# Value products that move 128 columns, and the next unit's pieces at the end of a step

## The reference, cut to what matters

```
L0  graph attention, 2 layers, 8 heads of 32:   out = softmax(leaky(self + neigh) + mask) @ feat
L0  causal attention inside the ffn, 16 heads of 16, and L3 attention, 16 heads of 16:  attn @ v
L1  latent attention, 16 heads, values of 64:   attn @ kv_rope
```

## Time and profile before

| | |
|---|---|
| median of 3 runs | 1486.96 us (1483.61 to 1492.53) |
| the profiled execution | 1486.61 us |
| its span, first to last instruction | 1484.8 us |
| PE busy, PEld busy | 1224.9 us (82%), 1031.5 us (69%) |
| DVE, ACT, POOL busy | 783.6, 595.3, 241.1 us |
| mean granted TensorE clock | 0.836 |
| graph attention's value products, L568 | 512 records, 106.2 us |
| small attention's, L872 | 768 records, 92.6 us |
| latent attention's, L1487 | 512 records, 60.5 us |

### The profile page before, as it was taken

How to read it: one execution, slowest core, us unless ns; L and a number is a source line. 1 busy time by engine, 2 the same in 40 slices (tenths; PEclk the granted TensorE clock), 3 DMA queues, 4 the chain that set the end, 5 groups by cost and what they waited for, 6 DMA issues and landing times. The chain is left out here.

```text
span 1484.8 us, 19438 instructions
## 1 busy us (share of the span) xinstructions
PE 1224.9 (82%) x7064; PEld 1031.5 (69%) x7064; DVE 783.6 (53%) x1966; ACT 595.3 (40%) x1032; POOL 241.1 (16%) x261
## 2 busy tenths in 40 slices
PE   6978888887998979989799799835267897979888
PEld 3546776676785867878589679734257685868777
DVE  2355434444756745544467457464564555744544
ACT  3335333442653733434244244211144553623433
POOL 2100000000404112334200000000023303012332
PEclk9976555656999988989899999966589998978999
DMA  8300000000000012223000000000022000012222
GB/s 331 95 2 2 1 1 1 2 1 0 2 1 1 2 53 76 84 87 100 26 1 1 1 1 2 3 2 4 0 80 63 1 1 0 2 62 75 75 87 79
DMA packets 19406, 52.17 MB, mean 35 GB/s; under 512 B 3504, under 2 KB 5808, under 8 KB 19184
## 3 DMA queue, kind: packets, MB, share of 16 engines
q1 hardware_dynamic: 19312, 50.93, 10.7%
HBM read 49.74 MB, written 1.05 MB: 34 GB/s over the span
## 5 line engine op out<-in xcount | busy, mean ns | idle before, releaser
L1098 POOL TENSOR_TENSOR p_WML<-p_raw,p_WMH 128x768 fp32r<-128x768 f32 (+1 forms) x78 | 135.1, 1735 | 256.9 <-ACT p_WMH L1200 251.3
L190 POOL TENSOR_SCALAR rstds<-mvs 128x4 f32<-128x4 f32 x16 | 3.7, 231 | 733.1 <-DVE mvs L185 484.1
L1258 ACT ACTIVATE p_AHI<-p_A 128x512 fp32r<-128x512 f32 x78 | 49.1, 629 | 177.5 <-DVE p_A L1399 177.4
L568 PEld LDWEIGHTS PS<-p_FT,p_PTS 128*128 128x128 f32 x512 | 105.9, 313 | 19.7 <-DVE p_PTS L748 17.7
L568 PE MATMUL PS<-p_FT,p_PTS 128*128 128x33 f32 x512 | 106.2, 381 | 11.9 <-ACT p_PTS L630 10.3
L79 PE MATMUL PS<-p_WMH,p_AHI 128*128 128x256 f32 x312 | 89.6, 287 | 13.5 <-DVE XS L1369 10.2
L1399 DVE TENSOR_TENSOR p_A<-p_A,PS 128x512 f32<-128x512 f32 x62 | 42.6, 688 | 108.3 <-PE PS L1154 108.0
L1403 DVE TENSOR_TENSOR p_ALO<-p_A,p_AHI 128x512 fp32r<-128x512 f32 x78 | 62.1, 796 | 67.4 <-ACT p_AHI L1258 65.3
L872 PEld LDWEIGHTS PS<-p_V,p_PTS 128*128 128x128 f32 x768 | 93.6, 197 | 0.0
L872 PE MATMUL PS<-p_V,p_PTS 128*128 128x17 f32 x768 | 92.6, 260 | 0.0
L748 DVE COPY p_PTS<-PS 128x512 f32<-128x512 f32 x32 | 22.1, 691 | 131.0 <-PE PS L581 131.0
(11 more groups left out here) (369 smaller groups left out, 3355.6 us busy)
## 6 DMA issues: line engine op xcount, KB each, us to landing
p_raw<-in_moe SPq DMA_DIRECT2D x62, 448.0 KB, 3.2
p_fr<-in_fold SPq DMA_DIRECT2D x16, 512.0 KB, 3.8
p_raw<-in_ffn SPq DMA_DIRECT2D x16, 320.0 KB, 2.9
p_raw<-in_wpack SPq DMA_DIRECT2D x8, 416.0 KB, 7.8
CP<-in_consts SPq DMA_DIRECT2D x1, 1725.0 KB, 12.3
XS<-in_x SPq DMA_DIRECT2D x1, 1024.0 KB, 15.3
out<-XS SPq DMA_DIRECT2D x8, 128.0 KB, 2.6
p_ctr<-in_ctxT SPq DMA_DIRECT2D x1, 512.0 KB, 16.1
```

The lines of the kernel that those rows point to most:

```text
L568: m = pe.matmul(PS[:, 6, hh * 33:hh * 33 + 33], PTS[:, n % 2, hh // 2, (hh % 2) * S + mt * P:(hh % 2) * S + mt * P + P], FT[:, u % 2, 2 * ...
L1098: g.tensor_tensor(WML[:, n % RING, :], raw[:, n % RAW, 0:SEL], WMH[:, n % RING, 0:SEL].bitcast(F32), ALU.subtract).then_inc(s["w_lo"], 1)
```

## The change

Widening: each value product moves 128 columns, with the used 17, 33 or 65 somewhere among them. The moving slice starts at the head's own columns where 128 fit behind them and otherwise ends with them, so the used part lies at the start or at the end of 128 result columns; four products fill one PSUM bank. DVE reads only the used columns. PE's first values wait for both parts of the ones columns, since the slice reaches over other heads.

Pieces: `STEP` is one lower for every piece. PE does `due(n)` at the end of step n instead of its beginning. ACT and DVE do `due(n - 1)` in step n: ACT ahead of `leaky(n + 2)` instead of behind it, DVE right behind `shift(n + 1)`, ahead of the copy of bank 4, instead of behind `elu`.

```diff
-                STEP = {"tr0": 2, "tr1": 3, "t": 4, "s": 5, "f0": 6, "f1": 7}
+                STEP = {"tr0": 1, "tr1": 2, "t": 3, "s": 4, "f0": 5, "f1": 6}
...
                             if n == 0:
-                                pe.wait_ge(s["ones"], 1)
+                                pe.wait_ge(s["ones"], 2)
...
-                                    m = pe.matmul(PS[:, 6, hh * 33:hh * 33 + 33], PTS[:, n % 2, hh // 2, (hh % 2) * S + mt * P:(hh % 2) * S + mt * P + P],
-                                                  FT[:, u % 2, 2 * (t // 2) + mt, 4 * hg + hh, :], start=(mt == 0), stop=(mt == 1))
+                                    lo = 33 * hh if hg == 0 else 33 * (5 + hh) - P
+                                    m = pe.matmul(PS[:, 6, hh * P:hh * P + P], PTS[:, n % 2, hh // 2, (hh % 2) * S + mt * P:(hh % 2) * S + mt * P + P],
+                                                  FT[:, u % 2, 2 * (t // 2) + mt].rearrange("p h o -> p (h o)")[:, lo:lo + P], start=(mt == 0), stop=(mt == 1))
...
                         for n in range(NN):
-                            for u, j in due(n):
-                                job(u, j)
                             if n:
                                 values(n - 1)
                             if n + 2 < NN:
                                 scores(n + 2)
                             weights(n)
+                            for u, j in due(n):
+                                job(u, j)
...
                             exps(n)
+                            if n:
+                                for u, j in due(n - 1):
+                                    if j[0] != "f":
+                                        high(u, j)
                             if n + 2 < NN:
                                 leaky(n + 2)
-                            for u, j in due(n):
-                                if j[0] != "f":
-                                    high(u, j)
...
-                            o = PS[:, 6, 0:132].rearrange("p (h o) -> p h o", h=4)
+                            at = 0 if hg == 0 else P - 33
+                            o = PS[:, 6, :].rearrange("p (h o) -> p h o", h=4)[:, :, at:at + 33]
...
                             if n + 1 < NN:
                                 shift(n + 1)
+                            if n:
+                                for u, j in due(n - 1):
+                                    low(u, j)
                             v.wait_ge(s["pt"], 2 * n + 1)
...
-                            for u, j in due(n):
-                                low(u, j)
...
-                                    at = (2 * qt + hh) * (HD + 1)
+                                    at = (2 * qt + hh) * P
+                                    hd = 2 * hp + hh
+                                    lo = hd * (HD + 1) if hd < 8 else (hd + 1) * (HD + 1) - P
...
-                                        m = pe.matmul(PS[:, 6 + n % 2, at:at + HD + 1], PTS[:, n % 2, hh, c * P:c * P + P],
-                                                      V[:, 2 * j + kt, 2 * hp + hh, :], start=(kt == 0), stop=(kt == qt))
+                                        m = pe.matmul(PS[:, 6 + n % 2, at:at + P], PTS[:, n % 2, hh, c * P:c * P + P],
+                                                      V[:, 2 * j + kt].rearrange("p h d -> p (h d)")[:, lo:lo + P], start=(kt == 0), stop=(kt == qt))
...
-                                        i = pe.matmul(PS[:, 6 + n % 2, at:at + DC + 1], PTS[:, n % 2, c:c + P],
-                                                      KV2[:, 2 * j + kt, DC:2 * DC + 1], start=(kt == 0), stop=(kt == 1))
+                                        i = pe.matmul(PS[:, 6 + n % 2, at:at + P], PTS[:, n % 2, c:c + P],
+                                                      KV2[:, 2 * j + kt, 1:2 * DC + 1], start=(kt == 0), stop=(kt == 1))
```

More of the change, by code:

```diff
@@ L1006, in outputs @@
                             v.wait_ge(s["pv"], n + 1)
-                            o = PS[:, 6 + b, 0:4 * (HD + 1)].rearrange("p (a d) -> p a d", a=4)
+                            at = 0 if hp < NH // 4 else P - HD - 1
+                            o = PS[:, 6 + b, :].rearrange("p (a d) -> p a d", a=4)[:, :, at:at + HD + 1]
                             v.reciprocal(rin[:, b, :], o[:, :, HD]).then_inc(s["rec"], 1)
@@ L1483, in values @@
                                 for hh in range(2):
-                                    at = (2 * qt + hh) * (DC + 1)
+                                    at = (2 * qt + hh) * P
                                     for kt in range(2):
                                         c = qt * 512 + hh * S + kt * P
-                                        i = pe.matmul(PS[:, 6 + n % 2, at:at + DC + 1], PTS[:, n % 2, c:c + P],
-                                                      KV2[:, 2 * j + kt, DC:2 * DC + 1], start=(kt == 0), stop=(kt == 1))
+                                        i = pe.matmul(PS[:, 6 + n % 2, at:at + P], PTS[:, n % 2, c:c + P],
+                                                      KV2[:, 2 * j + kt, 1:2 * DC + 1], start=(kt == 0), stop=(kt == 1))
                             i.then_inc(s["pv"], 1)
@@ L1590, in outputs @@
                             v.wait_ge(s["pv"], n + 1)
-                            o = PS[:, 6 + b, 0:4 * (DC + 1)].rearrange("p (a d) -> p a d", a=4)
+                            o = PS[:, 6 + b, :].rearrange("p (a d) -> p a d", a=4)[:, :, DC - 1:2 * DC]
                             v.reciprocal(rin[:, b, :], o[:, :, DC]).then_inc(s["rec"], 1)
```

## The result

The changed kernel takes 1381.61 us in the median (1380.92 to 1388.97, four runs), against 1489.74 for the kernel before in the same comparison: ratio 0.929, 95% interval 0.9243 to 0.9337. The forecast was 1409, the range 1386 to 1460. The profiled execution of after took 1380.92 us (span 1379.1), 105.7 us less than the profiled one of before.

A forecast was written before the change was run, and what follows sets the result against it. The graph stage was taken as bound by PE at its lower clock, small and latent attention by PE outright. 1486.6 - 96 (graph stage) + 18 (wide records) gave 1409 us, range 1386 to 1460.

The forecast's parts named there:

- The clock: Graph stage: wide value products raise PE's clock to the upper level after about two steps, and it stays.
- Rival 1: Graph stage: clock stays low, only piece waits go (-19 us), bill +18, 1486 us, no change; chance 0.08.
- rival 2: Graph stage: clock flickers, a third to half of 32 steps low, +28 to +46, 1437 to 1455 us; chance 0.15.
- The graph stage: Graph attention: 156 us against 252.4, so -96 us, with plain steps of 4.53 us and two low steps first.
- The move: Graph stage: moving ACT's and DVE's parts of pieces removes PE's waits; the first transposing piece still waits 0.7 us for elu.
- Rival 4: Graph stage: pieces do not gain, waits stay, +17 us, 1426 us; counted within the forecast's chance of 0.65.
- the 1.03 us: Graph step: time PE waits for the copies behind the transposes anyway; a piece costs only what exceeds it.
- both engines were idle where the pieces moved to: Graph stage: ACT and DVE idle there waiting for PE; one PE piece had waited 2.58 us for DVE's L674.
- The bill: Small and latent attention: wide records cost +11.9 and +6.1 us, together +18.0 (2 to 35).
- the stand-in: Wide record's full-clock price, taken from the 256-column fp32r product: 0.120 us, floor 0.107, upper bound 0.133.
- The narrow side: Price of a narrow value record at full clock: 0.1045 us in the small attention, 0.108 in the latent.
- PE has no idle time there: Small and latent attention: both PE-bound, so nothing hides the wide records' +18.0 us.

The follow-up runs named there:

- after: The changed kernel, all value products 128 columns and pieces moved, against the kernel before: 1381.61 us, ratio 0.929.
- wide_no_move: All value products 128 columns, pieces left where they stood in the kernel before: 1409.39 us, ratio 0.9461.
- gap_filler: Pieces moved, value products narrow, six bf16 products of 512 columns behind each graph step's transposes: 1402.04 us, ratio 0.943 against the kernel before.
- price run: Kernel before plus unused f32 products of 17 to 256 columns and fp32r of 128 and 256; f32 0.112 us a record at 17, 112 and 128 columns.
- act_behind: The changed kernel with ACT's part of a piece put back behind leaky: 1399.44 us, ratio 0.94 against the kernel before.
- as_changed: The changed kernel itself, unaltered, run again on another comparison's chip: 1384.28 us, ratio 0.93 against the kernel before.
- tuned: The changed kernel with latent attention at 65 columns again and twelve more products in the first graph step's waits: 1376.35 us, ratio 0.9248 against the kernel before.
- move_only: Pieces moved, all value products narrow as in the kernel before: 1429.94 us, ratio 0.9598.

## Why the prediction was wrong, point by point

**The clock: right, and a little late.** The step of the sum that everything hung on, that wide values raise the clock and hold it, is shown: by the width alone (wide_no_move, 178.2 us), by filler in its stead (gap_filler), and by the price run, where back-to-back narrow f32 records let it fall. The Trainium skill (TensorE: Matmul & The Clock Gate, "Why this matters for your kernels") asks for TensorE to be kept busy; the price run disagrees as far as the profile's busy time goes, 9.65 of 9.65 us busy at 0.51. That the engine mostly waits for weight loads in a narrow step fits this (17 and 128 columns cost the same 0.112 us), but no run measures the load by itself. The rise came in the first wide step, not after two. That was luck in part: in the same code it came in the second step of wide_no_move and in the third of act_behind. Rival 1, "clock stays low", and rival 2, "it flickers", did not come about, apart from one dip at steps 16 and 17 (6.10 and 5.66 us in after and as_changed), which tuned has not.

**The graph stage: 151.97 against 156.** Plain step 4.56 against 4.53, values 1.95 against 1.92; the one low step fewer gives -2.9 us, the part of the gain that was luck; the rest is the sum of small terms.

**The move: right in place, wrong in price.** The waits for L674, L681 and L688 went as forecast, but for one of 0.3 us; the one for elu is 1.5 us, not 0.7, in both units. Rival 4 priced their staying at +17; the runs say about 25, of which the waits are 23.5. That the 1.03 us, which I let each wait hide in, hid nothing is read from this sum and not tested by itself. And rival 1 priced the move at -19 with the clock low; move_only shows -60 in all, since without the pauses the clock rises in the piece steps by itself. This is the interplay that the prediction did not have: it treated clock and waits as two terms. That both engines were idle where the pieces moved to was right; that ACT's place is the one that counts most (some 15 of 25 us) was not said.

**The bill: the step that failed most.** "The nearest row with as many column passes is the 256-column fp32r product, 0.120": the stand-in was wrong. Its 0.120 belongs to fp32r of 256 columns; f32 of 128 columns costs 0.112, as much as 17 columns do. The narrow side was too cheap as well: 0.1045 and 0.108 are means over a group of records, whose first distance is 0.030 us (small) and 0.061 (latent) and whose others are 0.112, and a step got back part of what the group lost. Steps of 3.29 and 4.09 us instead of the 3.43 and 4.24 forecast: +4.5 us, not +18. That is 13.5 of the missing 28 us. With this price alone put right the forecast would be 1395, inside the range.

**The missing term.** What the wide values do behind the small attention was nowhere in the sum: I read "PE has no idle time there" and priced them as a pure cost. The earlier trace rows hardly shows it; the transposes at the ends of the calls would have, 1.78 to 1.94 us before where the upper level gives 1.04. The narrow records of the last two steps let the clock fall, and the transposes and the projection behind them ran low. Worth 9.8 us in this pair of traces (from +3.0 to -6.8), with the spread of 5 us named above. With 13.5 for the price, 4.4 for the graph stage, -0.5 for the latent's and 0.5 elsewhere these are the 27.7 us. The missing term takes the 1395 to 1385, just under the range, and the graph stage takes it to the 1381 measured.

## What to carry to other kernels

Where TensorE is busy in the records and low in its granted clock, look at what its records do: f32 products of a few columns cost as much as ones of 128 here, and the clock can fall under them. Columns that do not lengthen the record (here up to 128, at 0.112 us) are nearly free (4.5 us for 1280 records), and can buy the clock for the stage and for what stands behind it. Price an operation by a row of its own type and width; where only another has one, measure it. And when two traces differ, look first at the steps in which the code is the same: here the clock's rise alone moved a stage by 3 to 6 us.

When pauses and a low clock stand in the same stage, do not add their gains: taking either away shifts the other. And in an in-order queue put a side piece ahead of the instruction that waits longest, not behind it, where its input is there by then.

## What the runs showed of the hardware that I had not expected

With PE recorded busy 9.65 of 9.65 us, back-to-back f32 products of 64 and 96 columns, behind ones of 17, had a granted clock of 0.51, and back-to-back ones of 128 to 256 columns 1.00. By the median distance of their records, fp32r products cost 0.112 us at 128 columns and 0.120 at 256, and f32 0.112 at 17 and at 128 and 0.216 at 256. In the same code of the first graph steps the clock rose in the first step (after, 102.3 us), the second (wide_no_move, 110.2) or the third (act_behind, 117.9). Four products of 512 columns a step ahead of the scores left plain graph steps at the lower level, six in the wait behind the transposes held the upper one.
